# Two cross-attention layers on one core: SyncE issues the loads of context and of the next queries' rows at the end of a slot, and four pieces of one slot are ordered anew

## What is computed

```python
q = x @ Wq + bq;  k = ctx @ Wk + bk;  v = ctx @ Wv + bv      # 32 heads of 16; 8 heads of 16
scores = einsum('bkgld,bksd->bkgls', q, k) / sqrt(16) + mask
attn = softmax(scores, axis=-1)
out = einsum('bkgls,bksd->bkgld', attn, v) @ Wo + bo
x = layernorm(out + x) * gamma + beta
```

## Time and profile before

| | |
|---|---|
| median of three runs | 1801.05 us (1798.76 to 1801.15) |
| the profiled execution, its own time | 1800.77 us |
| its span in the profile | 1799.0 us |
| granted TensorE clock, mean over the span | 0.987 |
| busy: TensorE matmul, weight load, VectorE, ScalarE, GpSimd | 96%, 57%, 69%, 59%, 32% |
| 16 DMA engines | near half busy; 235.88 MB moved |

### The profile page before, as it was taken

One profiled execution on the slowest core, in us unless ns is written; L12 is line 12 of the kernel. 1 busy time (PEld: TensorE's weight loads), 2 busy tenths in 40 slices (PEclk: granted clock), 3 DMA queues, 4 the chain that ended last, 5 costly groups with the idle time before them and its releaser, 6 DMA issues. The chain is left out here.

```text
span 1799.0 us, 35959 instructions
## 1 busy us (share of the span) xinstructions
PE 1722.9 (96%) x11009; PEld 1020.6 (57%) x11009; DVE 1247.1 (69%) x1680; ACT 1056.7 (59%) x2402; POOL 584.3 (32%) x1165
## 2 busy tenths in 40 slices
PE   4899999999999999999999999999999999999997
PEld 3465566565566565565565565565566565565542
DVE  6476776677776676776677776677776677776674
ACT  1465565565665666665666665566666555665653
POOL 1233332333332333332333332333333332332321
PEclk8899999999999999999999999999999999999998
DMA  9455554454544554545554544544544454544531
GB/s 281 133 147 143 147 136 115 131 142 124 145 134 119 135 141 126 144 133 132 135 145 125 143 114 118 132 132 115 144 126 109 126 130 114 142 127 101 129 86 42
DMA packets 224986, 235.88 MB, mean 131 GB/s; under 512 B 73738, under 2 KB 199940, under 8 KB 224164
## 3 DMA queue, kind: packets, MB, share of 16 engines
q1 hardware_dynamic: 204452, 205.82, 42.1%
q10 hardware_dynamic: 20480, 29.38, 6.9%
HBM read 101.39 MB, written 22.02 MB: 69 GB/s over the span
## 5 line engine op out<-in xcount | busy, mean ns | idle before, releaser
L744 DVE TENSOR_REDUCE mx<-ms 128x2 f32<-128x750 f32 x896 | 818.7, 929 | 482.9 <-PE ms L871 477.4
L610 ACT ACTIVATE probs<-sc 125x448 f32<-125x448 f32 x1536 | 750.4, 541 | 295.1 <-PE sc L842 286.6
L871 PE MATMUL ms<-ks,qs 96*128 96x375 bf16 (+1 forms) x2560 | 439.1, 325 | 30.1 <-DMA qs<-qp 27.3
L842 PE MATMUL sc<-qs,ks 99*125 99x448 bf16 x1536 | 442.3, 361 | 15.1 <-DMA qs<-mT 9.5
L842 PEld LDWEIGHTS sc<-qs,ks 99*125 99x125 bf16 x1536 | 190.1, 136 | 241.0 <-ACT probs L610 136.0
L892 PE MATMUL pv<-probs,vs 125*32 125x448 f32 x3072 | 320.0, 550 | 0.0
L871 PEld LDWEIGHTS ms<-ks,qs 96*128 96x128 bf16 (+1 forms) x2560 | 176.5, 98 | 208.8 <-issue 71.0
L934 PE MATMUL job<-wo,on 128*112 128x512 f32 x512 | 264.3, 598 | 5.7 <-POOL on L519 5.7
L959 PE MATMUL job<-xT,wq 128*128 128x224 f32 x1024 | 216.2, 354 | 0.9 <-ACT qf L650 0.9
L758 DVE RECIPROCAL orec<-osum 128x112 f32<-128x112 f32 x256 | 214.3, 839 | 0.9 <-DMA osum<-oraw 0.9
L618 ACT COPY oraw<-pv 128x448 f32<-128x448 f32 x128 | 68.1, 532 | 246.6 <-PE pv L892 246.6
(11 more groups left out here) (54 smaller groups left out, 955.5 us busy)
## 6 DMA issues: line engine op xcount, KB each, us to landing
ctxT<-in_ctxT SPq DMA_DIRECT2D x64, 750.0 KB, 5.8
qs<-qp SPq DMA_DIRECT2D x768, 56.0 KB, 2.8
ks<-kp SPq DMA_DIRECT2D x768, 46.9 KB, 2.7
osum<-oraw ACTq DMA_DIRECT2D x128, 112.0 KB, 2.9
oc<-oraw ACTq DMA_DIRECT2D x128, 112.0 KB, 3.4
mask<-in_mask SPq DMA_DIRECT2D x64, 164.1 KB, 3.1
xT<-in_xT SPq DMA_DIRECT2D x32, 224.0 KB, 3.7
xin<-in_x SPq DMA_DIRECT2D x32, 224.0 KB, 6.0
```

Source lines behind the costliest of these rows:

```text
L610: nc.scalar.activation(probs[0:KCS, k, j, :], sc[j][0:KCS, 0:GL], ACT.Exp)\
L744: nc.vector.tensor_reduce(mx[o][:, cols], ms[n % 2][:, :, 0:S2], AX_X, ALU.max).then_inc(max_done[o], 1)
L842: last = nc.tensor.matmul(sc[j][0:KCS, 0:GL], ks[p][0:KM, g, rows], qs[p][0:KM, g, :], start=True, stop=not masked)
L871: last = nc.tensor.matmul(to, qs[o][0:KT, group, cols], ks[o][0:KT, group, :], start=True, stop=not masked)
```

## The change

Three entries of tables and the place of two loads change. The p = 0 slot finds its column maxima in piece 8 in place of 9 (`COLUMNS_AT`), casts the second part of the queries in piece 9 in place of 10 (`QUERY_REST_AT`), and has one maxima step less in piece 8 and one more in piece 9 (`STEPS_AT`). In every slot SyncE issues the load of `ctxT`, and in a p = 1 slot behind it the two of `xT`, after the last lot of `qs`.

```diff
-STEPS_AT = [[1, 1, 1, 1, 1, 1, 1, 1, 1, 1, 1, 1], [0, 1, 1, 1, 2, 1, 1, 1, 1, 1, 1, 1]]
+STEPS_AT = [[1, 1, 1, 1, 1, 1, 1, 1, 0, 2, 1, 1], [0, 1, 1, 1, 2, 1, 1, 1, 1, 1, 1, 1]]
...
-COLUMNS_AT = [(9, 3), (7, 2)]
+COLUMNS_AT = [(8, 3), (7, 2)]
...
-QUERY_REST_AT = [10, 6]
+QUERY_REST_AT = [9, 6]
...
                 if s_ok:
                     store_y(p, stored, lay[4])
-                if p == 1 and (not isinstance(proj, int) or 0 < proj + 1 < UNITS):
-                    after = lay[3] if not isinstance(proj, int) else 0 if proj + 1 < PER else 1
-                    for u in range(PAR):
-                        load_xT(u, proj + 1, after)
                 if isinstance(i, int):
                     next_layer(p, i)
-                if more and p == 0 and not (isinstance(ahead, int) and ahead + 1 == 0):
-                    load_ctx(o, ahead + 1, lay[3] if not isinstance(ahead, int) else 0 if ahead + 1 < PER else 1)
                 if m_ok:
                     load_x(p, main, lay[0])
                 if j_ok:
                     sp.wait_ge(k_p3[p], keys)
                     stack_terms(p, 0, ks[p], kp[p], 1)
-                if more and p == 1 and not (isinstance(ahead, int) and ahead + 1 == 0):
-                    load_ctx(o, ahead + 1, lay[3] if not isinstance(ahead, int) else 0 if ahead + 1 < PER else 1)
-                if j_ok:
                     sp.wait_ge(q_p1[p], queries)
                     stack_terms(p, 0, qs[p], qp, 0, of=(0,))
...
                     sp.wait_ge(q_p3[p], queries)
                     stack_terms(p, 0, qs[p], qp, 0, of=(2,))
+                if more and not (isinstance(ahead, int) and ahead + 1 == 0):
+                    load_ctx(o, ahead + 1, lay[3] if not isinstance(ahead, int) else 0 if ahead + 1 < PER else 1)
+                if p == 1 and (not isinstance(proj, int) or 0 < proj + 1 < UNITS):
+                    after = lay[3] if not isinstance(proj, int) else 0 if proj + 1 < PER else 1
+                    for u in range(PAR):
+                        load_xT(u, proj + 1, after)
```

More of the change, by code:

```diff
@@ L374, in slot @@
                     stack_terms(o, 1, ks[o], kp[o], 1)
-                if a_ok:
                     stack_terms(o, 1, qs[o], qp, 0)
```

## The result

| | before | changed |
|---|---|---|
| median, us | 1799.96 (4 runs, 1798.76 to 1801.15) | **1759.21** (4 runs, 1758.37 to 1760.43) |
| ratio | 1 | **0.9774**, 95% interval 0.9757 to 0.9791 |
| profiled execution, us | 1800.77 | 1758.37 |
| its span, us | 1799.0 | 1756.6 |

The change made the kernel 41 us faster.

What follows compares the result with a forecast made beforehand. The prediction took TensorE, 96% busy, as the bound, idle in the steady part almost only for SyncE's copies. Terms −25 + 3 + 0 − 2 = −24 us, against 1800.77 us, gave 1777 us, range 1768 to 1793.

Steps and rivals of the forecast that it cites:

- What bounds the kernel, and which copies are late: TensorE, 96% busy, bounds the kernel; the late copies are those SyncE issues at the end of the p = 1 slot.
- So I count the whole 25.0 us: Moving the p = 1 slot's three loads removes all TensorE's listed steady waits for `qs` and `mT`: −25 us.
- The lower end, −20: Same p = 1 waits, if landing time does not improve: 0.8 us of each wait goes, −20 us.
- only the issue counts: Rival: p = 1 slot's last `qs` still lands in 4.3 us, 20 us go, 1782 us; chance 0.69 together with the forecast.
- The context load in the p = 0 slot, +3: Behind the last `qs` it takes 6.3 us, so keys wait 0 to 0.2 us in 31 slots: +3 us (0 to +15).
- Pieces 8 to 10, 0 (−3 to +5): Two maxima steps in a row at the end of piece 9: a stall for a stall, 0, bounds −3 to +5 us.
- the sign that I named for trouble, idle for `mx`: VectorE's steps at the end of piece 9 would show as idle of L867 waiting for `mx`; no size given.
- The start, −2: First slots: of 4.9 us of waits for `mT` in the first 100 us, 2 us come back.
- What would show it: Profile after: waits for `qs` under 3 us, `mT` under 1; unit 53.3 us; p = 1 last `qs` lands in about 3.5.

Runs made afterwards that it cites:

- e10: Kernel before with the p = 1 slot's loads moved behind the last `qs`, plus a 4 KB load in the context's old place: 1772.25 us, ratio 0.9847.
- e3: Kernel before with only the three tables changed, SyncE's order as before: 1788.71 us, ratio 0.9953.
- e11: Changed kernel with the second maxima step of piece 9 moved into piece 10: 1762.73 us, ratio 0.9792.
- e6: Changed kernel with the old maxima table (`STEPS_AT`): 1767.55 us, ratio 0.9837.

## Why the prediction was off

- **What bounds the kernel, and which copies are late.** Right. e1 alone, which moves only the p = 1 slot's loads, shortens the span by 37.3 of 42.4 us.
- **"So I count the whole 25.0 us".** This step failed. The mechanism held and nearly all of the waits went (25.0 to 0.5 us), but the term was mis-sized: the waits cost 35.1 us, by the piece lengths. I took the idle column for the price of a wait, and it leaves out 0.16 us of each wait, the waits shorter than that, and a fall of the clock. The trace of before had the rows for it: scores at 651.25 and maxima at 653.08 (shown above) stand 1.83 us apart, where in an earlier piece, at 645.00 and 645.38, they stand 0.38 us apart with no wait.
- **The lower end, −20, and the rival "only the issue counts".** Wrong, since over 25 us went. The last `qs` is issued 1.0 us earlier in relation to the next slot's start in both layers, where I had 0.8: I took 0.42 us for the context load's issue, and with its waits it is 0.64. By e10 the bytes delay the landing by 0.6 us, where I had 0.8. But I had read the landing from one slot, 4.3 us, and the means were 3.7 and 3.5. The 3.5 us that I forecast were 2.8 in L0 and 3.65 in L1, where the gain thus came by the earlier issue.
- **The context load in the p = 0 slot, +3.** It was nothing. I took 6.3 us to land, and it was 5.2 at 558.64 and 4.1 to 6.4 in all places. The room was 6.8 us (issued at 558.64, keys at 565.60, less the 0.12 us) in place of the 6.1 to 6.6 that I gave it. The cast moved the end of the last `qs` by 1.4 us in relation to the keys (5.80 to 7.23 us ahead of them), not 0.7 to 1.2, and that `qs` lands in 2.4 us. The least that a context load had to spare in units 1 to 30 is 0.7 us. The Trainium skill ("DMA: Bandwidth & Descriptors", section "Anatomy of one DMA") has its fit for transfers that GpSimd issues, and I had used it for one of SyncE's: the estimate of 3.8 us is below the fastest load here, 4.1 us. The 0 that it gave for this term came true all the same.
- **Pieces 8 to 10, 0 (−3 to +5).** −1.6 us. It lies inside my bounds, and the sign that I named for trouble, idle for `mx`, appeared (6.0 us) without any cost.
- **The start, −2.** −2.3 us to the first score of unit 1, and the listed waits for `mT` in the first 100 us fell by 1.9. I left out the other end: the last unit and what follows gave 3.5 us more, 2.8 of them by the maxima table and the clock.
- **What would show it.** The waits fell as said, the last `qs` lands in 2.8 us in L0, and the unit is 53.2 us in L0, where I had said 53.3, but 52.6 in L1.

Sum by measured terms: units 1 to 30 −36.6 (−35.1 waits, −1.6 pieces 8 to 10, rounding), start −2.3, end −3.5, together −42.4 us of span. The −25 term in my sum was 10 us short, +3 should have been 0, pieces 8 to 10 gave 1.6, and the two ends 4 us more than I took: 18 us.

Not shown are what makes the landing of the same copy 2.8 us in one layer and 3.65 in the other, and how much of e3's gain in p0.0 is the tables'.

## What to carry to other kernels

Read the price of a wait as the distance between the starts of two instructions, against the same two where nothing is late, and take the idle column as a lower bound: here it showed 25 of 35 us. On one queue, put large loads behind the small copies that an engine waits for, if the place they move to has slack; measure that slack, since to be late there costs more than the lateness. Idle time that a reordering puts in front of another instruction need not be a cost, as e3 and e11 show. And look at the first and the last unit by themselves: here a table entry that is worth 0.07 us in a steady slot (e6) was worth 3 us in one piece of the last.

## What I had not expected of the hardware

**The clock falls after short waits too.** The kernel before, at the start of unit 29, windows as above:

```profile
1620.70:1622.00 1.30, 0.94 (x4) 0.19 (x2) 0.63 (x1) 0.16 (x1) 0.42 (x2) 1.00 0.95 167
1622.00:1624.00 2.00, 0.69 (x7) 0.22 (x10) 0.00 (x0) 0.98 (x2) 0.43 (x3) 1.00 0.47 120
1624.00:1626.00 2.00, 2.00 (x16) 0.61 (x19) 1.96 (x3) 0.00 (x0) 0.00 (x0) 0.66 0.25 80
1626.00:1628.00 2.00, 2.00 (x16) 0.60 (x12) 0.60 (x4) 0.00 (x0) 1.25 (x2) 0.50 0.27 88
```

And TensorE's timeline there:

```profile
1621.57 0.59 PE L842 MATMUL sc<-qs,ks 99*125 99x448 bf16 x2 [0.36 <-DMA qs<-mT]
1623.47 0.49 PE L871 MATMUL ms<-ks,qs 96*128 96x375 bf16 x2 [1.31 <-DMA qs<-qp]
1623.89 4.04 PE L892 MATMUL pv<-probs,vs 125*32 125x448 f32 x24
```

**Issue time.** Each of SyncE's small transfers of `ks` and `qs` takes it 0.59 to 0.64 us (3.78 for six), while the 750 KB of the context takes 0.38 us, not counting the waits ahead of it.
